# Cross-attention and feed-forward kernel: VectorE also adds pairs of key chunks for the third and fourth pair of heads of batches 1 to 3

## What is computed

```python
lat = layer_norm(layernorm(x)); ctx = layer_norm(context)
q = heads(lat @ Wq); k = rope(heads(ctx @ Wk)); v = heads(ctx @ Wv)
attn = clip(einsum("bhnd,bhsd->bhns", q, k) * DHEAD ** -0.5, -11.0, 11.0)
attn = softmax(attn, axis=-1)                       # over s, the 512 keys
x = x + einsum("bhns,bhsd->bhnd", attn, v) @ Wo + bo
# second layer: h = rmsnorm(layernorm(x)); attention of each token's 16 heads with each other; gate; experts
x = x + second_layer(x)
```

## Time and profile before

| what | value |
|---|---|
| median of three runs | 329.18 us |
| the profiled execution, whole | 329.66 us |
| its span, first to last instruction | 327.5 us |
| TensorE matmul busy | 300.6 us, 92% of the span |
| VectorE busy | 249.7 us, 76% |
| GpSimd busy | 207.9 us, 63% |
| ScalarE busy | 159.8 us, 49% |
| mean granted TensorE clock | 0.958 of full speed |
| the chain that ended last, by engine | PE 48%, DVE 28%, POOL 7%, issue 7%, ACT 4% |
| `sums` from `e`, on the page | 384 records, 23.2 us busy |
| `add_chunks` of batch 0, on the page | 16 instructions, 11.9 us busy |

### The profile page before, as it was taken

The page is one execution under the profiler, slowest core; times in us unless marked ns, Lnnn a source line. Parts: engine busy times, 40 slices in busy tenths (PEclk is TensorE's granted clock), DMA queues, the critical chain, the costliest instruction groups (busy, mean ns, idle before and its releaser), DMA issues.

```text
span 327.5 us, 6571 instructions
## 1 busy us (share of the span) xinstructions
PE 300.6 (92%) x2464; PEld 206.5 (63%) x2464; DVE 249.7 (76%) x476; ACT 159.8 (49%) x300; POOL 207.9 (63%) x206
## 2 busy tenths in 40 slices
PE   6859999999999999998999999999999988979685
PEld 5736666666668766665787665557776754755531
DVE  2956898675884849999877899965677798759936
ACT  2534645667443736554436347745335556122430
POOL 5525695665572839596627577698557765978461
PEclk9795999999999999999999999999999999999957
DMA  7843122211210101112101111111110100000001
GB/s 217 238 118 99 41 50 63 68 34 40 52 32 10 47 20 36 31 34 51 25 22 34 35 32 34 32 35 32 34 26 25 35 0 2 2 16 0 1 0 34
DMA packets 16319, 14.24 MB, mean 43 GB/s; under 512 B 4832, under 2 KB 11808, under 8 KB 16288
## 3 DMA queue, kind: packets, MB, share of 16 engines
q1 hardware_dynamic: 15232, 13.69, 15.8%
q10 hardware_dynamic: 1056, 0.13, 0.3%
HBM read 4.89 MB, written 0.52 MB: 17 GB/s over the span
## 4 chain that ended last, share of the span: by engine, by line
PE 48%; DVE 28%; POOL 7%; issue 7%; ACT 4%; DMA 3%; SPq 1%; ACTq 0%; POOLq 0%; DVEq 0%
PE pv L617 10%; PE sc L603 10%; PE sums L638 5%; PE side L710 3%; PE pj_k L541 3%; DVE ks L1100 3%; DVE own_bank L1269 2%; PE pj_k L543 2%; PE pj_k L542 2%; DVE prod L1055 2%; POOL e L1637 2%; ACT e L856 2%; DMA sin_in<-in_L_xattn_sin_dram 2%; DVE ksin L1164 2%; DMA kswap<-ksin 2%
## 5 line engine op out<-in xcount | busy, mean ns | idle before, releaser
L1637 POOL TENSOR_SCALAR e<-e 128x1024 f32<-128x1024 f32 x64 | 70.9, 1108 | 69.6 <-ACT e L856 65.1
L856 ACT ACTIVATE e<-sc 128x1024 f32<-128x1024 f32 x64 | 65.6, 1025 | 32.9 <-PE sc L603 32.9
L603 PEld LDWEIGHTS sc<-qs,ks 64*128 64x128 f32 x768 | 51.3, 191 | 26.3 <-issue 24.2
L603 PE MATMUL sc<-qs,ks 64*128 64x256 f32 x768 | 64.4, 301 | 3.0 <-ACT e L856 2.9
L617 PE MATMUL pv<-e,v 128*64 128x256 f32 x512 | 62.3, 385 | 0.0
L1630 POOL TENSOR_TENSOR krot<-kcos,kswap 128x512 f32<-128x512 f32 x32 | 44.2, 1383 | 11.2 <-DMA kswap<-ksin 8.7
L617 PEld LDWEIGHTS pv<-e,v 128*64 128x64 f32 x512 | 33.9, 136 | 23.1 <-issue 6.9
L864 ACT ACTIVATE u<-pv 128x256 f32<-128x256 f32 x32 | 12.3, 385 | 61.5 <-PE pv L617 61.5
L1100 DVE TENSOR_TENSOR ks<-krot,ks 128x512 fp32r<-128x512 f32 x32 | 31.0, 968 | 0.0
L1164 DVE TENSOR_TENSOR ksin<-pj_k,sinT 128x512 f32<-128x512 f32 x32 | 21.9, 686 | 6.0 <-POOL krot L1630 3.6
L638 PE MATMUL sums<-e,sum_rows 128*32 128x256 f32 x384 | 23.2, 382 | 1.2 <-POOL e L1637 1.2
(11 more groups left out here) (280 smaller groups left out, 581.6 us busy)
## 6 DMA issues: line engine op xcount, KB each, us to landing
kswap<-ksin SPq DMA_DIRECT2D x128, 64.0 KB, 2.0
ctx_in<-in_ctx_dram SPq DMA_DIRECT2D x4, 256.0 KB, 3.0
prod<-in_L_xattn_Wkv_dram SPq DMA_DIRECT2D x2, 512.0 KB, 6.9
x_in<-in_x_dram SPq DMA_DIRECT2D x1, 512.0 KB, 6.7
prod<-in_L_xattn_Wq_dram SPq DMA_DIRECT2D x1, 512.0 KB, 7.5
wo<-in_L_xattn_Wo_dram SPq DMA_DIRECT2D x1, 512.0 KB, 7.0
fwe<-in_L_ffn_We_dram SPq DMA_DIRECT2D x1, 512.0 KB, 4.1
out_dram<-x_in SPq DMA_DIRECT2D x3, 128.0 KB, 1.8
```

What stands on the lines that cost most here:

```text
L603: last = nc.tensor.matmul(sc[:, h, c * NT:(c + 1) * NT], ks[rows, j % 3, k_part, chunk], qs[rows, j % 2, q_part, :], start=(k_part + q_par ...
L856: nc.scalar.activation(e[:, j % 3, :, 2 * half:2 * half + 2, :].rearrange("p h c n -> p h (c n)"), sc[:, :, :], ACT.Exp, scale=SCALE).then ...
L1637: nc.gpsimd.tensor_scalar(a, a, EXP_HIGH, EXP_LOW, ALU.min, ALU.max).then_inc(s_clip, 1)
```

## The change

`chunks_added(j)` says for which pairs VectorE adds chunks. It was `j < PAIRS`, batch 0 alone; now it also holds for the third and fourth pair of every later batch: j = 10, 11, 18, 19, 26, 27. For these `add_chunks` runs twice per pair (half 0 at the end of slot j, after the second layer's steps, half 1 at the start of slot j + 1, before `key_products`), and writes into `e_added_later`, which is the tile `on` under another shape. That tile holds the normalised attention outputs and is last read by `out_proj` in slots 10, 18 and 26. `sums(11)`, `sums(19)` and `sums(27)` read two results per head and wait for the adds.

```diff
+def chunks_added(j):
+
+    return j < PAIRS or j % PAIRS in (2, 3)
...
+        e_added_later = on.rearrange("p k n -> p (k n)").rearrange("p (j c h n) -> p j c h n", j=2, c=2, h=2)
...
+        def added_of(pair):
+            return e_added if pair < PAIRS else e_added_later
...
-                if j < PAIRS:
+                if chunks_added(j):
                     n = 2
-                    pe.wait_ge(s_added, 2 * j + 2)
+                    pe.wait_ge(s_added, 2 * sum(chunks_added(i) for i in range(j + 1)))
...
-                                                e_added[:, pair % 2, c, g % 2, :] if j < PAIRS
+                                                added_of(pair)[:, pair % 2, c, g % 2, :] if chunks_added(j)
...
-                nc.vector.tensor_tensor(e_added[:, j % 2, half, :, :], e[:, j % 3, :, 2 * half, :],
+                nc.vector.tensor_tensor(added_of(j)[:, j % 2, half, :, :], e[:, j % 3, :, 2 * half, :],
...
-                if 1 <= slot <= PAIRS:
+                if 1 <= slot <= NPAIR and chunks_added(slot - 1):
                     add_chunks(slot - 1, 1)
...
-                if 0 <= slot < PAIRS:
+                if 0 <= slot < NPAIR and chunks_added(slot):
                     add_chunks(slot, 0)
```

## The result

The changed kernel is slower. Over six executions each its median is 336.14 us (331.32 to 338.17) against 328.98 us (328.41 to 331.42) for the kernel before. That the changed kernel is slower is clear; whether by over 2% is not. The forecast was 334.4 us, ratio 1.016. In some executions of the changed kernel, the profiled one among them (337.43 us, span 335.6 us), TensorE's clock falls in the middle of the work; that profile can't be read without this, and a second profile of the same program, in which the clock held, is shown beside it further down.

A forecast was written before the change was run, and what follows sets the result against it. TensorE was taken to bound the middle of the kernel. Batch 1's gain of 0.1 us and losses of 2.55 and 2.75 us gave +5.2 us on the median of 329.18: 334.4 us, range 330.5 to 336.5 us.

The forecast's parts named there:

- TensorE sets the time, and the shorter sums gain 0.87 us each: Mid-kernel, TensorE hardly stands still; three sums shrink by 0.87 us each, so 2.6 us is the most gained.
- Two adds and GpSimd take turns, for whole instructions: VectorE's pairs of adds and GpSimd each wait for the other's whole instruction; this case, 333.0 to 335.2 us, had 55%.
- Batch 2 loses 2.55 us, batch 3 2.75 us: Sums of pairs 19 and 27 wait for adds behind `root_norm`; the values product starts at 185.5 instead of 182.96 in batch 2.
- Idle time near 2.9 us ahead of the sums: TensorE in slots 20 and 28 would stand about 2.9 us waiting for VectorE's adds, and almost none in slot 12.
- the lateness of `ks`: Batch 2: `ks` falls behind GpSimd's clip, slot 20's scores start some 0.5 us late, inside the longer stall, adding nothing.
- `rr` and the end of `root_norm` 0.25 us late: Batch 2: GpSimd's `rr` follows the delayed clip about 0.25 us later, so `root_norm` ends at 181.8 instead of 181.57.
- Batch 1 gains 0.1 us: Pairs 10 and 11, without `root_norm`: sums start 0.75 us late but are 0.87 us shorter; bounds 0.87 gain, 0.5 loss.
- The clock: Rival: TensorE's clock falls behind the stalls in slots 20 and 28, 1.6 us each; 336 or 337.6 us; chance 13%.
- Its only gap of that size before: TensorE's 2.54 us gap ahead of 309.18, with granted clock 0.80 around it; TensorE was thinly used there.
- The other side, faster, if `root_norm` were not ahead: Rival: adds done before the sums are due gain 2.6 us, 326.6 us; `root_norm` ahead prevents it; faster or level 6%.

The follow-up runs named there:

- e1: Kernel before, but the sums of pairs 11, 19 and 27 read only two chunks and no adds are made: ratio 0.997, stretches 2.41 us shorter in all.
- e5: Changed kernel with GpSimd's bias addition (`xl`) in slots 12, 20 and 28 moved behind both clips: the three stretches +5.28 us in all against the kernel before.
- e3: Changed kernel with both adds of pairs 19 and 27 put ahead of `root_norm` on VectorE: ratio 0.996 against the kernel before.
- e8: Changed kernel run again unaltered, for a second profile and more executions: ratio 1.016 against the kernel before, executions from 331.12 to 336.62 us.
- e4: Changed kernel with 12 identity matmuls on TensorE ahead of the sums of pairs 19 and 27: ratio 1.011, executions from 329.7 to 335.2 us.
- e2: Changed kernel, but the sums of batches 1 to 3 read four chunks, don't wait, and the adds go unused: ratio 1.011 against the kernel before.

## Why the prediction was right

- **TensorE sets the time, and the shorter sums gain 0.87 us each.** Right: 1.86 us became 1.00 us, and e1's stretches gain 0.90, 0.66 and 0.85.
- **Two adds and GpSimd take turns, for whole instructions.** Right, and tested: the pair took 2.67 us with `xl` and the clip pending, 2.12 with the clip alone (e5), 1.28 beside nothing that holds it (e3). So these two engines wait for each other where no semaphore asks for it, which the section on the kernel before leaves out.
- **Batch 2 loses 2.55 us, batch 3 2.75 us.** Right: they lost 2.47 and 2.74 us with the clock held (e8), 2.44 and 2.65 with TensorE kept busy (e4).
- **Idle time near 2.9 us ahead of the sums.** It was 2.63 and 2.79. The rest came earlier: TensorE was already late when it reached the sums, as the prediction had it for `ks`, but the first cause in batch 2 was one that I didn't name, the bank `side` that VectorE emptied late (0.73 us). In batch 3 it was another unnamed one, the low part of the queries (`qs`, a wait of 0.71 us). As I wrote of the lateness of `ks`, both are swallowed by the longer wait behind them; they show by themselves in e2. e2's second wait, at `keyval2`, doesn't come up in the changed kernel, where TensorE gets there 2.5 us late anyhow.
- **`rr` and the end of `root_norm` 0.25 us late.** It was 0.12 us: `root_norm` ended at 180.68, 20.36 us behind the sums of slot 18, where the kernel before has 20.24.
- **Batch 1 gains 0.1 us.** It gained 0.33 to 0.37. The step that failed is the order beside the adds of pair 11, with the lateness of TensorE, which was 0.51 us at the sums and not 0.75. I let `krot` run ahead of the first add. But `rotate` waits for `s_klo` of the pair two before, that is for `ks` itself, so it could not be pending yet. The first add went through at once, then `krot`, then the second add, and the pair was done at 114.22, ahead of the sums at 114.66. `xl` came behind both.
- **The clock.** I gave its fall 13%, at 336 us for one and 337.6 us for two. The first profile had two falls and took 337.43 us, e8's had none and took 331.12 us. The chance was too small: three of six executions lay above 337 us. The price was 1.6 us each, for an assumed 4 us at the lower level. Batch 3 paid 1.5 us and batch 2 2.9 us, where the clock stayed at the lower level about twice as long with work to do (0.50 from 184 to 188 us and 0.64 from 188 to 190, against 0.50 from 258 to 260 and 0.72 from 260 to 262). Two grounds for the small chance were wrong. "Its only gap of that size before" misses a longer one in the same profile, where the kernel starts:

```profile
24.27 0.79 PE L541 MATMUL pj_k<-ctxT,wkA 128*128 128x512 f32 x1 [2.79 <-DVE kcos L1164]
```

The granted clock is 1.00 ahead of it, from 20 to 22 us, and 0.50 from 24 to 32 us. In all ten profiles here a gap of 2.77 or 2.79 us stands at this place, and in all ten the clock falls to 0.50 in it or within 3 us behind it. And TensorE being full on both sides of the gap did not keep the clock up in slots 20 and 28 of the first profile.

- **How far the number was luck.** Without the clock, the forecast of +5.2 us stands beside +4.9 us, and that agreement was worked out. The whole time was not: the median of all executions, 336.14 us, is 1.7 us above the forecast of 334.4 and just inside the range that ends at 336.5, a range that left out two falls, the very case of the first profile. That the ratio of 1.0165 meets the forecast of 1.016 comes from leaving out the three longest executions. How much of the 1.7 us is due to falls in slots 20 and 28 and how much to the start and the tail is open, since only two executions have a profile.
- **The other side, faster, if `root_norm` were not ahead.** That condition was the right one: e3 moves only the adds of pairs 19 and 27 ahead of it, and its stretches are 0.7 us shorter than those of the kernel before.

## What to carry to other kernels

Work moved off the busiest engine pays only if its new place is behind nothing that waits: here the change cost 4.9 us with the clock held, because four of its twelve adds stood behind `root_norm`, and gained 1.9 us with all twelve in idle time of the same engine a few steps earlier. Where two engines got in each other's way as VectorE and GpSimd do here, price a run of VectorE's adds with one whole GpSimd instruction in front of each as long as GpSimd has a large one pending. A tiny one didn't count: beside GpSimd's `rr`, of two columns, both adds of e3 took 0.68 us. When executions differ by more than the effect, compare stretches between groups of instructions that the change leaves alone: that of batch 1 repeated within 0.04 us over the five profiles whose code is the same there, while whole times of one kernel moved by 6 us.

## What the runs showed of the hardware beyond expectation

The same idle time of TensorE, 2.63 us with full work on both sides, was followed by a fall to 1.2 GHz in one execution and by none in another of the same program. Nor did it go by the length: in e5 a gap of 2.13 us was followed by a fall (0.50 from 182 to 184 us), and one of 2.25 us by none. In e4, with 24 small matmul records in the gap, the clock held, but as it also held without them in e8, one profile doesn't show that they protect it. What a fall cost didn't follow the length of the stall ahead of it: 2.9 us behind 2.63 us in one place, 1.5 us behind 2.79 us in the other.

VectorE's adds held up by GpSimd ended a fixed time behind the end of GpSimd's instruction: 0.54 us in the changed kernel and in e5, 0.55 in batch 0 and in slot 12, where an add takes 0.69 alone. An estimate from these: about 0.14 us of an add passes while it waits. GpSimd's were lengthened in the same way: the clip took 1.04 us alone, 1.36 with one add in front of it and 1.50 in e5.
